# Queries spread to the edges in rounds over two banks, part of the projection ahead of them, target rows by transfers

## The reference

```python
h = relu(layernorm(x));  x = x + gcn(h, W0, b0)        # layer 0
h = relu(layernorm(x))                                 # then twice, elu between them:
xr = einsum('nd,rdf->rnf', h, W)                       # projection, 3 relations
oi, oj = xr[etype, dst], xr[etype, src]
alpha = leaky_relu(oi @ q + oj @ k, 0.2)               # query of the target, key of the source
e = exp(alpha - segment_max(alpha, dst)[dst])
a = e / (segment_sum(e, dst)[dst] + 1e-16)
out = segment_sum(a * oj, dst) + b;   x = x + out      # x + out after layer 2
```

## Time and profile before

| | |
|---|---|
| median of 3 runs | 1668.91 us |
| the profiled execution's own time | 1667.57 us |
| its span, first to last instruction | 1665.8 us |
| mean granted TensorE clock | 0.931 of full speed |
| PE busy | 1522.1 us (91%) |
| POOL busy | 1047.0 us (63%) |
| DVE busy | 954.8 us (57%) |
| ACT busy | 254.8 us (15%) |
| bytes moved | 265.90 MB, 160 GB/s over the span |

### The profile page before, as it was taken

The page is one execution under the profiler, slowest core; times in us unless marked ns, Lnnn a source line. Parts: engine busy times, 40 slices in busy tenths (PEclk is TensorE's granted clock), DMA queues, the critical chain, the costliest instruction groups (busy, mean ns, idle before and its releaser), DMA issues.

```text
span 1665.8 us, 26774 instructions
## 1 busy us (share of the span) xinstructions
PE 1522.1 (91%) x6490; PEld 893.2 (54%) x6494; DVE 954.8 (57%) x2323; ACT 254.8 (15%) x621; POOL 1047.0 (63%) x1170
## 2 busy tenths in 40 slices
PE   4988999999988997999879999957999999899996
PEld 2454545555556554666545555524555566455553
DVE  8577744454552888889858887620643553223332
ACT  2544311111110111011000022340111011000000
POOL 1488276666525887888267777605777773577673
PEclk9988999999995998899979999985999999899999
DMA  8300388887732122111178888740123122789897
GB/s 299 122 20 20 114 304 288 256 265 239 224 74 60 49 61 94 30 40 40 39 228 288 298 269 267 221 141 2 44 54 106 40 50 48 237 299 304 280 301 271
DMA packets 86506, 265.90 MB, mean 160 GB/s; under 512 B 32619, under 2 KB 32994, under 8 KB 86438
## 3 DMA queue, kind: packets, MB, share of 16 engines
q0 software_dynamic: 51840, 199.49, 39.1%
q1 hardware_dynamic: 34598, 65.57, 11.0%
...
## 4 chain that ended last, share of the span: by engine, by line
PE 69%; POOL 12%; issue 7%; DVE 5%; DMA 4%; ACT 1%; DVEq 1%; POOLq 0%; SPq 0%; PEld 0%; PEldq 0%; ACTq 0%
PE ps L1219 14%; PE ps L1190 12%; PE ps L1259 12%; POOL ring L473 9%; PE ps L1261 6%; PE ps L1262 6%; PE ps L1085 5%; PE ps L1125 3%; PE ps L1128 2%; PE ps L1145 2%; DMA ring<-rows,idxr 2%; PE ps L1035 2%; PE ps L1006 1%; PE ps L1048 1%; DVE zw L922 1%
## 5 line engine op out<-in xcount | busy, mean ns | idle before, releaser
L1219 PE MATMUL ps<-wreg,hT 128*128 128x384 f32 x1440 | 485.4, 499 | 7.3 <-PEq L1212 6.6
L473 POOL DMA_INDIRECT ring<-keys,idxr x360 | 382.5, 1063 | 173.8 <-issue 103.6
L444 POOL DMA_INDIRECT ring<-rows,idxr x304 | 304.0, 1000 | 178.4 <-PEq L1247 65.8
L1219 PEld LDWEIGHTS ps<-wreg,hT 128*128 128x128 f32 x1440 | 280.0, 196 | 201.6 <-issue 22.3
L1190 PE MATMUL ps<-ring,zw 128*128 x664 | 233.7, 496 | 3.6 <-DVE zw L816 3.5
L1259 PE MATMUL ps<-ring,zw 128*128 x664 | 224.1, 496 | 13.3 <-DVE zw L983 13.1
L444 POOL DMA_INDIRECT ring<-rows,idx x152 | 147.2, 968 | 109.4 <-PE ps L1190 75.5
L917 DVE TENSOR_TENSOR hn<-hn,al 128x1024 f32 (+1 forms) x166 | 137.8, 830 | 128.8 <-POOL al L486 90.0
L1259 PEld LDWEIGHTS ps<-ring,zw 128*128 128x128 f32 x664 | 125.9, 192 | 108.2 <-issue 38.8
L981 DVE TENSOR_TENSOR ring<-ring,al x166 | 159.4, 960 | 40.4 <-SPq L362 25.1
L1190 PEld LDWEIGHTS ps<-ring,zw 128*128 128x128 f32 x664 | 113.3, 190 | 78.6 <-issue 34.5
...
## 6 DMA issues: line engine op xcount, KB each, us to landing
wreg<-in_L_gnn_W SPq DMA_DIRECT2D x11, 2304.0 KB, 9.9
...
xs<-in_x SPq DMA_DIRECT2D x3, 1152.0 KB, 13.5
...
```

The source lines that it names most:

```text
L444: nc.gpsimd.indirect_dma_start(ring[:, t % (2 * RING), 0:WIDTH[l]], None, rows[l], bass.IndirectOffsetOnAxis(idx[:, t:t + 1], 0)).then_inc ...
L473: nc.gpsimd.indirect_dma_start(kb[:, n % KSEMS, t % KB, 0:4], None, keys[l], bass.IndirectOffsetOnAxis(idxr[:, t:t + 1], 0)).then_inc(k_in ...
L1219: last = mm(ps[:, 2 * (nt % 2) + h, 0:HALF], hT[:, k, nt * P:(nt + 1) * P], wreg[:, r % 2, k, h * HALF:(h + 1) * HALF], start=(k == 0), st ...
```

## The change

**Target rows by transfers.** The loop of layer 0 no longer makes, turns and copies `s16`. Instead PE turns the table of targets (two products) before layer 0, ACT copies it, SP writes it to memory as one row of 180 x 128 bf16, and ACT's queue loads this row into all 128 partitions of `stT` in six loads (`ST_LOADS`), 46 KB a partition, 5.9 MB in all. DVE turns it into one-hots in place, in 12 parts of 1920 elements (`ST_PARTS`), two after each of the node tiles 3 to 8 of layer 0 (`ST_AT`).

**Rounds.** `spread_queries` takes 4 pairs (8 edge tiles) a round, into one of two banks in turn; ACT copies each round out (`keep_queries`); PE waits with a round until the copy two rounds back is done. DVE then masks and adds from `qe`, after the last copy. Which of the banks a round has is computed in registers, from the bounds, by `chunk_of` and `chunk_shifts`.

**Projection ahead.** 3 half tiles of layer 1 and 5 of layer 2 (`AHEAD`) are projected before the queries are spread, between the last turns of node tiles; PE goes on with the others right behind the spread. The key table is stored at another place of SP's program, the ones of `stage` are set earlier, and the q and k vectors of layer 2 are loaded again for the third relation.

**Sums opened by eight columns.** `open_acc` multiplies zeros over 8 columns instead of 386.

```diff
+CHUNK = 4
+QW = 16
+BANK_Q, BANK_M = 6, 6
+AHEAD = {1: 3, 2: 5}
...
+ST_LOADS, ST_PARTS, ST_AT = 6, 12, {3: (0, 1), 4: (2, 3), 5: (4, 5), 6: (6, 7), 7: (8, 9), 8: (10, 11)}
...
+        def chunk_shifts(eng, bnd):
+            shift = [0]
+            for j in range(NT):
+                shift.append(eng.snap(shift[j] + (bnd[j + 1] * (CHUNK - 1) + bnd[j]) % CHUNK))
+            return shift
+        def chunk_of(i, shift):
+            return (i + shift) // CHUNK
...
+            sp.wait_ge(tlT_in, 2)
+            row = targets_row.rearrange("(t p) -> t p", p=P)
+            sp.dma_start(row[0:P, :], tlT[:, 0, :]).then_inc(s_targets, 16)
+            sp.dma_start(row[P:T, :], tlT[0:T - P, 1, :]).then_inc(s_targets, 16)
...
+                        if n == l - 1:
+                            store_keys(l)
+                        if l == 1 and n == 1:
+                            sp.wait_ge(wq2_done, R)
+                            load_weights(1, 1)
...
+            act.wait_ge(wq_copied, R)
+            act.wait_ge(s_targets, 32)
+            act.wait_ge(s_rows0, 16 * (NT + 1))
+            act.wait_ge(stage_ones, 1)
+            n = T * P // ST_LOADS
+            for a in range(ST_LOADS):
+                act.dma_start(stT[:, a * n:(a + 1) * n], targets_row[a * n:(a + 1) * n].partition_broadcast(P)).then_inc(s_targets, 16)
...
+            def keep_queries(l):
+                w = R * HEADS[l] if HEADS[l] > 1 else 3 * R
+                for j in range(NT):
+                    if j >= 1:
+                        act.wait_ge(q_read[l], chunk_of(bnd[j], shift[j]) + 2)
+                    with act.Fori(bnd[j], bnd[j + 1], CHUNK) as i:
+                        c = chunk_of(i, shift[j])
+                        act.wait_ge(q_chunk[l], c + 1)
+                        nc.scalar.activation(qe[:, ds(i * (2 * w), 2 * CHUNK * w)].rearrange("p (t x) -> p t x", x=w),
+                                             ps[:, ds(c % 2 + BANK_Q, 1), 0:2 * CHUNK * QW].rearrange("p o (t x) -> p (o t) x", x=QW)[:, :, 0:w], ACT.Copy).then_inc(q_read[l], 1)
+                act.wait_ge(q_read[l], chunk_of(bnd[NT], shift[NT]) + 2)
+                act.sem_inc(q_spread[l], 1)
...
-            for j in range(NT + 1):
-                if j < NT:
-                    with act.Fori(bnd[j], bnd[j + 1]) as i:
-                        act.wait_ge(st_ready, i + 2)
-                        nc.scalar.activation(stT[:, ds(i * PAIR, PAIR)], ps[:, ds(i % 2 + 6, 1), 0:P].bitcast(BF16), ACT.Copy).then_inc(st_copied, 1)
...
+                keep_queries(l)
+                for n in range(AHEAD[l], 2 * R * NT):
+                    keep_projected(l, n)
...
+                    keep_projected(2, 0)
+                    keep_projected(2, 1)
                     node_tile(NT - 1)
+                    keep_projected(2, 2)
                     keep_by_query(2, NT // 2 - 1)
+                    keep_projected(2, 3)
+                    keep_projected(2, 4)
...
-                            dve.wait_ge(st_ready, i + 1)
-                        V.tensor_scalar(s16[:, b, :], iota_h[:, 0:P], tl[:, ds(t, 1)], None, ALU.is_equal).then_inc(o16_in, 1)
...
+                if j in ST_AT:
+                    dve.wait_ge(s_targets, 32 + 16 * ST_LOADS)
+                    n = T * P // ST_PARTS
+                    for a in ST_AT[j]:
+                        V.tensor_scalar(stT[:, a * n:(a + 1) * n], stT[:, a * n:(a + 1) * n], iota_p[:, 0:1], None, ALU.is_equal).then_inc(st_ready, 1)
...
+                if H > 1:
+                    picked = qe[:, 0:T * R * H].rearrange("p (t r h) -> p t r h", r=R, h=H)
+                    link(V.tensor_tensor(picked, picked, rmask[:, :, :].unsqueeze(3).to_broadcast([P, T, R, H]), ALU.mult))
+                    V.tensor_reduce(qs[:, 0:T * H].rearrange("p (t h) -> p t h", h=H), picked.rearrange("p t r h -> p t h r"), AX.X, ALU.add).then_inc(rows_go[l], 1)
...
-                    mm(ps[:, 2 * (j % 2) + a, 0:HALF + 2], zero16[:, 0:P], zero16[:, 0:HALF + 2], start=True, stop=False, skip_group_check=True)
+                    mm(ps[:, 2 * (j % 2) + a, 0:8], zero16[:, 0:P], zero16[:, 0:8], start=True, stop=False, skip_group_check=True)
...
+            def spread_queries(l):
+                pe.wait_ge(q16_ready, l)
+                pe.wait_ge(st_ready, 1 + ST_PARTS)
+                pe.wait_ge(g_in[l - 1], (bnd[NT] + (RING - 1)) // RING * (2 * RING) + (RING + 1))
+                pe.sem_inc(q_read[l], 2)
+                w = R * HEADS[l]
+                for j in range(NT):
+                    with pe.Fori(bnd[j], bnd[j + 1], CHUNK) as i:
+                        c = chunk_of(i, shift[j])
+                        pe.wait_ge(q_read[l], c + 1)
+                        for k in range(2 * CHUNK):
+                            o = ps[:, ds(c % 2 + BANK_Q, 1), k * QW:(k + 1) * QW].rearrange("p o c -> p (o c)")
+                            onehot = stT[:, ds(i * PAIR + k * P, P)]
+                            if HEADS[l] == 1:
+                                last = mm(o[:, 0:3 * w].rearrange("p (c q) -> p c q", c=3), onehot, q16[:, j, :, 0:w], start=True, stop=True)
+                                continue
+                            for part in range(3):
+                                last = mm(o[:, 0:w], onehot, q16[:, j, part, 0:w], start=(part == 0), stop=(part == 2))
+                        last.then_inc(q_chunk[l], 1)
...
+            def project(l, first, end):
+                H = HEADS[l]
+                for n in range(first, end):
+                    r, nt, h = n // (2 * NT), n % (2 * NT) // 2, n % 2
+                    if n == 0:
+                        pe.sem_inc(stage_in[l], 4)
+                    if n % (2 * NT) == 0:
+                        pe.wait_ge(s_w[l], r + 1)
+                    if n == 2 * NT:
+                        pe.wait_ge(q_spread[l], 1)
+                        spread_open(BANK_M, SM)
+                    if n in (0, 2):
+                        pe.wait_ge(acc_free[l - 1], NT - 1 + n // 2)
+                    pe.wait_ge(stage_in[l], n + 1)
+                    for k in range(KT):
+                        last = mm(ps[:, 2 * (nt % 2) + h, 0:HALF], hT[:, k, nt * P:(nt + 1) * P], wreg[:, r % 2, k, h * HALF:(h + 1) * HALF], start=(k == 0), stop=(k == KT - 1))
+                    last.then_inc(p_ready, 1)
...
-                            if b == 1:
-                                pe.wait_ge(o16_in, 2 * i + 2)
-                                pe.wait_ge(st_copied, i + 1)
-                                for c in range(2):
-                                    last = nc.tensor.transpose(ps[:, ds(i % 2 + 6, 1), 0:P].bitcast(BF16).rearrange("p o c -> p (o c)")[:, c * P:(c + 1) * P], s16[:, c, :], ident16[:, :])
-                                last.then_inc(st_ready, 1)
...
+            project(1, 0, 1)
+            by_query(1, NT // 2 - 1)
+            project(1, 1, 2)
+            by_node(1, NT // 2 - 1)
+            project(1, 2, 3)
...
-                spread_open(BANK_Q, SQ)
-                for j in range(NT):
-                    spread(j, q16, BANK_Q, R * H, SQ)
-                spread_close(BANK_Q, SQ, q_spread[l])
-                pe.wait_ge(spread_read, 2 * l - 1)
...
+                spread_queries(l)
+                project(l, AHEAD[l], 2 * R * NT)
+                spread_close(l)
...
+                    project(2, 0, 1)
+                    to_features(2, NT - 2)
+                    project(2, 1, 2)
+                    by_node(2, NT // 2 - 2)
+                    to_features(2, NT - 1)
+                    project(2, 2, 3)
+                    by_query(2, NT // 2 - 1)
+                    project(2, 3, 4)
+                    by_node(2, NT // 2 - 1)
+                    project(2, 4, 5)
```

232 lines of the change are left out of this document (111 added, 121 removed).

## The result

The changed kernel takes 1718.25 us (median of 5 runs, 1714.51 to 1727.82) against 1667.62 us of the kernel before (5 runs): a ratio of 1.0309, 95% interval 1.0291 to 1.0328. It is slower by 51 us, where 29 were forecast, and lies 2 us above the range.

The account below looks back on a forecast made before the run. Each stage had its own bound: TensorE in layer 0, register sets in the spreads, GpSimd in layer 1's projection. Terms -4.4 + 20 + 17 - 4 = +28.6 gave 1696.2, about 1697 us against the median; range 1670 to 1716.

Parts of the forecast that it names:

- layer 0: First layer's pair loop: -15.9 us from dropped work, +4.5 for in-place one-hots, +7 for target-row loads; together -4.4 us.
- the range: Whole kernel, 8 in 10: 1670 to 1716 us, leaving out the all-cheap rounds case and the dearest rounds.
- the 0.8 that stands ahead: Start of the kernel: two turns of the target table and two ACT copies cost 0.8 us.
- a ring that covers half of 14 us: Layer 0's gather ring of 8 tiles hides about half of the 14 us of target-row loads: +7 us.
- the opens: Opening sums with 8 columns instead of 386: -1.5 us in layer 0, -2 each in layers 1 and 2.
- one-hots in place: Twelve VectorE operations in layer 0, 0.74 us each, exposed at three of six node tiles: +4.5 us.
- start of layer 1's spread: Half tiles projected ahead between layer 0's last turn and layer 1's first round delay the spread: +7.0 us.
- the queue behind the weights: Entering layer 2, queries and turns queue behind a half tile waiting for weights; first one-hot later: +9 us.
- the rounds: Query spreads of layers 1 and 2: 25 rounds of 1.87 us plus extra register sets, +13.5 us a spread.
- The extra sets of L1210: Register sets growing by node tile in the spread's rounds, 39 over all rounds: +6.2 us a spread.
- rival (2): Spread rounds take 2.6 us because ACT handshake and L1210 divisions precede each round's first product: 1720 us; chance 0.13.
- forecast case: Whole kernel as the main sum has it, 1682 to 1712 us, rounds of 1.7 to 2.1 us; chance 0.62.

Follow-up runs that it names:

- second profile: The changed kernel run once more with nothing edited, to get another profile: 1717.01 us, ratio 1.0294 to the kernel before; profiled span 1711.6 us.

## Why the prediction was wrong

**Near in the sum, by luck: layer 0.** Its last turn came 4.0 us earlier (forecast 4.4). But 1.9 of this lie ahead of the first open, which fell anywhere from 212.9 to 218.3 us in the profiles. From there to the last turn the sum had -5.2 (without the 0.8 that stands ahead); the profiles of this layer 0 on the fast chips have 260.4 to 264.9 us, against 262.4 before: -2.1 to +2.5. Pairs run at 2.59 us, as foretold. TensorE idled 8.4 us under the loads (forecast 7, by a ring that covers half of 14 us), the opens gave nothing that shows (forecast 1.5), and one fall of the clock cost 1.7 us (forecast nothing).

The Trainium skill (Trainium Kernel Development and Optimization, "Key Constraints") says that transfers of the SP, ACT and POOL queues share 16 DMA engines and interleave. The trace agrees: in the changed layer 0 VectorE waits 3.9 to 4.2 us at a time for gathers while the loads of another queue run. With the loads issued one by one, and all other edits, TensorE waits 3.4 us for VectorE up to 293 us, instead of 7.5 to 9.5.

**Right: one-hots in place.** 715 ns each (723 in the second profile) against 0.74 us forecast. The Trainium skill (VectorE: DVE Perf Modes, "The perf-mode tier table (the rule you actually need)") would give 0.65 us, an estimate from 693 ns for 2048 elements; the trace is 10% above. The wait grew by 1.63 us at three node tiles, 4.9 against 4.5; of each 1.63, 0.39 shows behind node tile 2 too, where there are no one-hots (0.92 instead of 0.53), so they cost 3.7. Not in the sum was the clock. Behind these longer waits it fell at one place of three in the second profile and at all three in the first, and cost 1.6 to 1.7 us each time.

**Right: start of layer 1's spread,** +6.9 against +7.0 (the forecast's own terms give 6.8), and **the queue behind the weights,** +8.3 against +9.

**Failed: the rounds,** in one term. "The extra sets of L1210 ... 39 over all rounds: +6.2" took each set at 0.16 us, the price of a set with an address for one one-hot. They cost 12.0 and 13.0 us, shown by the run that computes each shift once. The wrong step was to count sets: the time went by the operations in them, some 0.04 us each and four more a node tile, and these also filled the set of L1208, which the forecast did not count as grown. The rest of the round was right: 1.90 us against 1.87. Both spreads reach the end in full, as forecast (the run with each shift once is 26 us faster), so the miss of 6.9 and 6.1 us (13.0) is most of the 17.4 us between sum and trace. The list of instructions showed how full the sets were; the trace of before had a row for another kind of set only.

**Failed: the opens.** -1.5 in layer 0 and -4 behind it, against nothing (0.9994 to 1.0017). The text said that many lie beside waits; the row of 0.53 us wait ahead of a first pair was the evidence for every second node tile of layer 0. In the sums of layers 1 and 2, +0.4 twice instead of -2 twice: 4.8 us. With 13.0 these are 17.8, against the 17.4 to be explained. That the account closes so well is in part luck, since the sums of layer 1 alone differ by up to 8.6 us between profiles, and with opens alone changed they were 1.9 us shorter.

**Failed: the range.** It took the rounds as one unknown of 1.7 to 2.1 us and gave the dear end to rival (2) (2.6 us for "handshake" and the divisions of L1210, 1720). That rival was half right: the mean round was 2.38 us in layer 1, by the operations of L1208 and L1210; the handshake costs nothing, as doubled copies showed. With the 13 us on top of the forecast case's own 1712 the range would have reached 1725.

What stays open: how the 0.04 us of an operation divide between modulo or division and the rest; what decides whether the clock falls behind a wait of 2.2 us; how much of the half tiles ahead and of the turns reaches the end on its own, since the intervals of these two runs overlap that of the kernel they stand on; and why the slower chips pause TensorE.
